# Residual half added on VectorE, plain first gathers, and inverse deviations placed between the second gathers

## What is computed

```python
x = layernorm(x + attention(x))             # causal, ALiBi bias, RMSNorm on q, k and y, then Wproj
logits = x @ w_router                       # 2048 x 8
top_vals, top_idx = top_k(logits, 2)
probs = softmax(top_vals)
for every token and each of its two experts e, with its weight p:
    out += p * (square(relu(x @ w_fc[e])) @ w_proj[e])
x = layernorm(x + out)                      # (v - mean) / sqrt(var + 1e-5)
```

## Time and profile before

| | us |
|---|---|
| median of 3 timed runs | 1530.89 (1529.89 to 1531.99) |
| the profiled execution, its own time | 1529.72 |
| its span in the trace | 1528.0 |
| PE busy in the span | 1430.8 (94%) |
| DVE busy | 770.4 (50%) |
| ACT busy | 728.5 (48%) |
| POOL busy | 421.3 (28%) |
| mean granted TensorE clock | 0.974 of full speed |

### The profile page before, as it was taken

The page is one execution under the profiler, slowest core; times in us unless marked ns, Lnnn a source line. Parts: engine busy times, 40 slices in busy tenths (PEclk is TensorE's granted clock), DMA queues, the critical chain, the costliest instruction groups (busy, mean ns, idle before and its releaser), DMA issues. The chain is left out here.

```text
span 1528.0 us, 26403 instructions
## 1 busy us (share of the span) xinstructions
PE 1430.8 (94%) x8000; PEld 1216.7 (80%) x8001; DVE 770.4 (50%) x1784; ACT 728.5 (48%) x1633; POOL 421.3 (28%) x417
## 2 busy tenths in 40 slices
PE   7999999999999999999999999699999579999980
PEld 5888888888888888888888887588888468888870
DVE  6555555655555655655555555345545433333323
ACT  5655565655655655656555655222222123333333
POOL 1221212212221221221212211143233333443376
PEclk9999999999999999999999999899999789999995
DMA  4112111021111121111111120735455266556499
GB/s 154 51 39 62 35 54 62 28 62 48 41 62 48 41 62 48 41 48 62 41 48 62 37 74 21 271 146 206 160 183 181 102 214 237 202 193 246 138 180 206
DMA packets 71979, 160.24 MB, mean 105 GB/s; under 512 B 14096, under 2 KB 14736, under 8 KB 69520
## 3 DMA queue, kind: packets, MB, share of 16 engines
q1 hardware_dynamic: 61168, 109.56, 21.7%
q0 software_dynamic: 10784, 50.36, 10.9%
HBM read 107.37 MB, written 52.52 MB: 105 GB/s over the span
## 5 line engine op out<-in xcount | busy, mean ns | idle before, releaser
L312 POOL TENSOR_TENSOR small<-small,half 128x4 f32<-128x4 f32 x193 | 194.6, 1008 | 764.5 <-DVE small L341 764.5
L264 ACT ACTIVATE prob<-logit,small 128x128 f32<-128x128 f32 (+3 forms) x256 | 144.2, 563 | 119.7 <-DVE small L413 117.0
L413 DVE CUSTOM_DVE_ANT_0 logit<-score_ps,bias 128x128 f32<-128x128 f32 (+3 forms) x256 | 124.8, 488 | 142.9 <-PE score_ps L506 142.5
L520 PEld LDWEIGHTS y_ps<-vs,prob_t 128*128 128x128 f32 x1280 | 174.8, 191 | 22.4 <-ACT prob_t L271 4.6
L520 PE MATMUL y_ps<-vs,prob_t 128*128 (+1 forms) x1280 | 185.2, 275 | 1.0 <-ACT prob_t L271 0.7
L271 ACT ACTIVATE prob_t<-prob_ps 128x128 f32<-128x128 f32 (+3 forms) x256 | 111.5, 436 | 53.4 <-PE prob_ps L513 52.3
L740 ACT ACTIVATE yt_hi<-turn_ps,subln 128x512 fp32r<-128x512 f32 x64 | 44.0, 688 | 170.4 <-PE turn_ps L1005 166.3
L513 PE MATMUL prob_ps<-ident,prob 128*128 128x128 f32 x640 | 112.7, 274 | 3.2 <-ACT prob L264 3.2
L1014 PE MATMUL out_ps<-w_hi,yt_hi 128*128 128x512 f32 x256 | 107.7, 421 | 6.4 <-DVE yt_lo L846 6.4
L465 PE MATMUL k_ps<-w_hi,x_hi 128*128 (+1 forms) x256 | 103.5, 404 | 6.2 <-DVE w_lo L373 6.2
L465 PE MATMUL v_ps<-w_hi,x_hi 128*128 (+1 forms) x256 | 106.7, 417 | 0.0
(11 more groups left out here) (169 smaller groups left out, 3284.7 us busy)
## 6 DMA issues: line engine op xcount, KB each, us to landing
y_scratch<-x_now SPq DMA_DIRECT2D x65, 256.0 KB, 2.9
x_raw<-in_x_t SPq DMA_DIRECT2D x64, 256.0 KB, 2.8
y_raw<-y_scratch SPq DMA_DIRECT2D x15, 1024.0 KB
w_raw<-in_w_experts POOLq DMA_DIRECT2D x7, 2048.0 KB, 8.3
w_hi<-in_w_experts POOLq DMA_DIRECT2D x7, 2048.0 KB, 8.4
w_raw<-in_w_all SPq DMA_DIRECT2D x16, 768.0 KB, 5.7
slots_y<-zeros SPq DMA_DIRECT2D x13, 768.0 KB
xs<-slots_x SPq DMA_DIRECT2D x39, 256.0 KB
```

Source lines behind the costliest of these rows:

```text
L264: nc.scalar.activation(prob[:, 0:width], logit[:, 0:width], ACT.Exp, scale=-1.0, bias=least[:, h:h + 1], accum_out=row_sum[:, (i % 2) * HG ...
L312: nc.gpsimd.tensor_tensor(r, ms, half[:, :], ALU.pow).then_inc(ready, 1)
L413: nc.vector.tensor_tensor_reduce(out=logit[:, 0:width], in0=score_ps[:, 0:width], in1=bias[:, h, T - width:T], scale=1.0, scalar=3e38, op0 ...
L520: mm = nc.tensor.matmul(y_ps[:, h * D:(h + 1) * D], prob_t[:, j * P:(j + 1) * P], one(vs[:, bass.ds(now, 1), j, h * D:(h + 1) * D]), start ...
```

## The change

Everything is computed at half scale in the resident path, so that the two halves add up in the slot outputs.

- Residual block: POOL's L801 becomes one instruction `(var + eps) * 4`, with a nop before it, so the normalised tile is halved. The `eps` tile and its memset go. The exponential of the second weight takes scale 2, and the gates are multiplied by 4 (through 0.25 in `either`), since the halved input gives a quarter after the square. ACT's copy into `x1` (L747) goes; DVE's `layernorm` waits for `x1_turned` in place of `x1_kept`.
- End of the residual block: dispatch(15) stands before send_gates(14) in POOL's program.
- Expert block: `xs` has four buffers with a semaphore each. The first four row loads wait no more for PE. Later loads are issued after the store of `yo(k)`, where they stood ahead of the wait for it. POOL waits for all four first loads before it goes on to expert 1's `w_hi`.
- ACT's scaled copy into `yo` goes; DVE computes `yo = ye * gate + xs`, last in its step.
- The first gathers have no `compute_op`. The second gathers add as before.
- The inverse deviations are made four tiles at a time after the issue of second gathers 6, 10 and 14, for the tiles 0 to 3, 4 to 7 and 8 to 11, and at the end for 12 and 13, and for 14 and 15. DVE's L1361 follows the same grouping.

```diff
-                out = x1[:, t, :] if isinstance(t, int) else one(x1[:, bass.ds(t, 1), :])
-                nc.scalar.activation(out, x1_now[:, b, :], ACT.Copy).then_inc(x1_kept, 1)
...
-                nc.gpsimd.tensor_tensor(var_eps[:, :], mean_var[:, 1:2], eps[:, :], ALU.add).then_inc(var_biased, 1)
+                pool.nop(nofuse=True)
+                nc.gpsimd.tensor_scalar(var_eps[:, :], mean_var[:, 1:2], EPS, 4.0, ALU.add, ALU.mult).then_inc(var_biased, 1)
...
             dispatch(NT - 2, 0)
+            dispatch(NT - 1, 1)
             send_gates(NT - 2, 0)
-            dispatch(NT - 1, 1)
             send_gates(NT - 1, 1)
...
-        xs = sb("xs", [P, 2, C])
+        xs = sb("xs", [P, YB, C])
...
-                at = tile_at(k)
-                if k >= 2:
-                    sp.wait_ge(xs_turned, k - 1)
-                load_rows(at, k % 2)
+                load_rows(tile_at(k), k)
...
-                if more(k, 4):
-                    sp.wait_ge(xs_turned, k + 3)
-                    sp.nop(nofuse=True)
-                    load_rows(at, b)
                 sp.wait_ge(yo_ready, k + 1)
                 sp.nop(nofuse=True)
                 out = y_slots[k] if isinstance(k, int) else rows_of(y_slots[bass.ds(k, 1), :, :])
                 sp.dma_start(out, yo[:, y, :]).then_inc(yo_stored[y], 16)
                 if more(k, 4):
+                    load_rows(at, y)
                     load_gates(at, y)
...
-            for b in range(2):
-                pool.wait_ge(xs_loaded[b], 16)
+            for y in range(YB):
+                pool.wait_ge(xs_loaded[y], 16)
...
-                                        bass.IndirectOffsetOnAxis(ap=slot_y[:, 0, t:t + 1], axis=0),
-                                        compute_op=ALU.add).then_inc(first_gathered, 16)
+                                        bass.IndirectOffsetOnAxis(ap=slot_y[:, 0, t:t + 1], axis=0))\
+                    .then_inc(first_gathered, 16)
...
+                if t in AFTER:
+                    inverse_std(t - RB - 2, t - 2)
+            for t in (NT - 4, NT - 2):
+                inverse_std(t, t + 2)
...
-                act.wait_ge(down_done, k + 1)
-                act.wait_ge(yo_stored[y], q * 16 + 16)
-                act.wait_ge(g_loaded[y], q * 16 + 16)
-                nc.scalar.activation(yo[:, y, :], ye_ps[b][:, :], ACT.Copy, scale=gs[:, y:y + 1]).then_inc(yo_ready, 1)
...
+                dve.wait_ge(down_done, k + 1)
+                dve.wait_ge(yo_stored[y], q * 16 + 16)
+                dve.wait_ge(g_loaded[y], q * 16 + 16)
+                nc.vector.scalar_tensor_tensor(yo[:, y, :], ye_ps[b][:, :], gs[:, y:y + 1], xs[:, y, :],
+                                               ALU.mult, ALU.add).then_inc(yo_ready, 1)
```

More of the change, by code:

```diff
@@ L752, in second_weight @@
                 src = gap[:, t:t + 1] if isinstance(t, int) else gap[:, bass.ds(t, 1)]
-                nc.scalar.activation(second[:, b:b + 1], src, ACT.Exp).then_inc(second_ready, 1)
+                nc.scalar.activation(second[:, b:b + 1], src, ACT.Exp, scale=2.0).then_inc(second_ready, 1)
             act.wait_ge(early_loaded, 32)
@@ L1118, in expert_phase @@
         we_loaded = sem("we_loaded")
-        xs_loaded = [sem("xs_loaded0"), sem("xs_loaded1")]
+        xs_loaded = [sem(f"xs_loaded{y}") for y in range(YB)]
         xs_turned, xt_rounded, xt_ready = sem("xs_turned"), sem("xt_rounded"), sem("xt_ready")
@@ L1247, in _, with inverse_std @@
                 pool.indirect_dma_start(x1[:, t, :], None, slots_y,
[L1248 to L1249 removed]
+                                        bass.IndirectOffsetOnAxis(ap=slot_y[:, 0, t:t + 1], axis=0))\
+                    .then_inc(first_gathered, 16)
             stored_up_to(E - 1)
             pool.wait_ge(first_gathered, 16 * NT)
+            def inverse_std(first, last):
+                pool.wait_ge(var_biased, last)
+                nc.gpsimd.tensor_tensor(rstd[:, first:last], var_eps[:, first:last], half[:, 0:last - first], ALU.pow)\
+                    .then_inc(rstd_ready, last - first)
+            pool.wait_ge(set_up, 1)
             for t in range(NT):
@@ L1255, in _ @@
                                         compute_op=ALU.add).then_inc(second_gathered[t], 16)
-            pool.wait_ge(set_up, 1)
-            for t in range(NT):
-                if t % 2 == 1 and t < NT - 2 or t >= NT - 2:
-                    n = 2 if t < NT - 2 else 1
-                    part = slice(t + 1 - n, t + 1)
-                    pool.wait_ge(var_biased, t + 1)
-                    nc.gpsimd.tensor_tensor(rstd[:, part], var_eps[:, part], half[:, 0:n], ALU.pow)\
-                        .then_inc(rstd_ready, n)
+                if t in AFTER:
+                    inverse_std(t - RB - 2, t - 2)
+            for t in (NT - 4, NT - 2):
+                inverse_std(t, t + 2)
         @block.scalar
@@ L1357, in bias_variance, with scale_mean @@
                     .then_inc(var_biased, 1)
-            def scale_mean(t):
-                dve.wait_ge(rstd_ready, t + 1)
-                nc.vector.scalar_tensor_tensor(minus_mean[:, t:t + 1], mean_var[:, t, 0:1], -1.0, rstd[:, t:t + 1],
-                                               ALU.mult, ALU.mult).then_inc(mean_ready, 1)
+            def scale_mean(first, last):
+                dve.wait_ge(rstd_ready, last)
+                nc.vector.scalar_tensor_tensor(minus_mean[:, first:last], mean_var[:, first:last, 0], -1.0,
+                                               rstd[:, first:last], ALU.mult, ALU.mult).then_inc(mean_ready, last - first)
             for t in range(NT):
@@ L1373, in _, with turn_x @@
             bias_variance(NT - 1)
-            for t in range(NT - 3, NT):
-                scale_mean(t)
+            for t in (NT - 4, NT - 2):
+                scale_mean(t, t + 2)
         @block.tensor
         def _(pe):
-            def turn_x(b, loaded):
-                pe.wait_ge(xs_loaded[b], loaded)
+            def turn_x(b, y, loaded):
+                pe.wait_ge(xs_loaded[y], loaded)
                 for c in range(CT):
-                    mm = nc.tensor.transpose(xt_ps[b][:, c * P:(c + 1) * P], xs[:, b, c * P:(c + 1) * P], ident[:, :])
+                    mm = nc.tensor.transpose(xt_ps[b][:, c * P:(c + 1) * P], xs[:, y, c * P:(c + 1) * P], ident[:, :])
                 mm.then_inc(xs_turned, 1)
```

37 lines of the change are left out of this document (18 added, 19 removed).

## The result

The changed kernel takes 1550.61 us (median of four runs, 1549.22 to 1554.26), the kernel before 1531.44 beside it: a ratio of 1.0136 with an interval of 1.0123 to 1.0149. It is 1.3% slower where 0.2% faster was forecast, and outside the range. The profiled execution has a span of 1547.6 against 1528.0, 19.6 more.

What follows compares the result with a forecast made beforehand. PE was taken to bound nearly everything, gathers and statistics the last 46 us. Slots 5.2 us later (2.5 + 2.7), yet second gathers 3.9 earlier; with 0.4 more tail, -3.5 us in sum: 1527.4 us, range 1523.5 to 1533.

Steps and rivals of the forecast that it cites:

- meeting point: End of the residual block: two POOL DMAs moved behind dispatch(15) make POOL's wait there end 2.5 us later.
- `w_hi`(1) late, with the boundary: Start of the expert block: POOL's wait for four row loads issues expert 1's `w_hi` 7.6 us late, plus the boundary's 2.5.
- chain late at expert 5, with the boundary: POOL's weight chain recovers 2.4 us and is 5.2 us late at expert 5, plus the boundary's 2.5.
- PE's stall for `w_lo` at tile 22: Expert 5's first tile: PE has 2.2 us of slack and stands 2.7 us for the late low parts.
- waits for rows: SP's later row loads in the slot steps: cost taken as 0, bound 1.5 us.
- tile 31 stored late: Slot tiles at the end of the expert block: 5.2 us late, from 2.5 at the boundary and 2.7 of PE's stall.
- plain gather, step: First gathers on POOL: 1.3 us a step without the addition, bounds 1.3 and 1.85.
- slot steps beside the gathers: Last slot tiles while POOL issues first gathers: no added time was counted.
- store of tile 35 to second gathers: The store of tile 35 ends last ahead of the second gathers, which start 2.89 us after it.
- tail: Start of the second gathers to the end: 46.6 us against 46.2, three POOL pauses included; bounds 45.5 and 49.
- dear plain gathers: Rival: POOL's plain first gathers cost as much as adding ones, 1.85 us each; say 1535.1 us, chance 0.13.
- DVE's addition: DVE's three-operand operation in each slot step: 0.75 us, hidden; without cover 0.75 on each of 39 tiles.

Runs made afterwards that it cites:

- a_freewait: The changed kernel with a wait that is always met ahead of every first gather; 1539.54 us in one run.
- b_plain: The kernel before with one edit, first gathers without the addition (residual missing from the result); 1537.35 us, ratio 1.0051.
- a_win8_alone: The changed kernel with one edit: first gather t waits until gather t-8 has landed; 1540.08 us in one run.
- a_onewait: The changed kernel with a single wait, ahead of first gather 8, for the landing of gather 0; 1537.78 us in one run.
- b_half: The kernel before with plain first gathers that bring rows of half the width; span 1520.2 us in one run.
- b_tail: The kernel before with inverse deviations for six, four and three tiles behind second gathers 10, 13 and 15, then one and two; 1528.64 us, ratio 0.9987.
- a_win4: The changed kernel with first gather t waiting for gather t-4's landing, gates of tile 14 before dispatch(15), a wait for two row loads and b_tail's grouping; 1525.02 us, ratio 0.9955.
- a_paced: The changed kernel with a one-column power on POOL behind each plain first gather, 1.86 us a step; 1538.65 us, ratio 1.0051.
- a_pace_short: The changed kernel with a 0.2 us sum on POOL behind each plain first gather, 1.37 us a step; 1550.84 us, ratio 1.0129.
- a_burst4: The changed kernel, but after every fourth first gather POOL waits until all issued ones have landed; 1547.27 us in one run.
- a_order: The changed kernel with send_gates(14) ahead of dispatch(15) again, as before the change; 1548.36 us, ratio 1.0112.
- a_win6: As a_win4, but first gather t waits until gather t-6 has landed; 1525.37 us in one run.
- a_win8: As a_win4, but first gather t waits until gather t-8 has landed; 1524.49 us in one run.
- a_nowin: a_win8 without its waits between the first gathers, its other edits kept; 1529.39 us in one run.
- a_add: The changed kernel with adding first gathers again, onto zeros that ACT writes; 1541.9 us, ratio 1.0070.

## Why the prediction was wrong

| step | forecast | measured |
|---|---|---|
| meeting point | +2.5 | +3.1 |
| `w_hi`(1) late, with the boundary | 10.1 | 10.9 |
| chain late at expert 5, with the boundary | 7.7 | 9.6 |
| PE's stall for `w_lo` at tile 22 | 2.7 | 1.8 (PE's bracket: 1.57) |
| waits for rows | 0 | 2.1 and 0.6 |
| tile 31 stored late | 5.2 | 8.0 (11.2 to 13.9 in six others) |
| plain gather, step | 1.3 | 1.26 |
| slot steps beside the gathers | unchanged | +14.4 |
| store of tile 35 to second gathers | 2.9 | 2.9 |
| tail | 46.6 | 52.5 |

Added up against the forecast's span (1528.0 - 3.5 = 1524.5): 2.8 for the slots ahead of the gathers, 14.4 for the standstill and 5.9 for the tail are 23.1, and 1524.5 + 23.1 = 1547.6. In a_freewait, without the standstill, the excess over the forecast is 13.3 us: 6.9 for the slots, 0.9 between the store of tile 35 and the second gathers, 5.5 for the tail (52.1). So the forecast fails with and without the standstill.

- *What held.* The rival "dear plain gathers" was wrong: they take 0.95 us, and b_plain shows the same. The end of the wait at the meeting point does follow the last issue: 7.1 us, where I took 6.1. What ends last ahead of the second gathers is the store of tile 35, as I said. DVE's addition takes 0.75 and is hidden in the slot steps (not at their end, see the tail). The Trainium skill's rule (page "SBUF — State Buffer", "Who interferes with whom"), by which a VectorE instruction with at most one SBUF input, outside the two-port modes, does not contend with GpSimd, agrees with the traces: POOL's eight subtractions take 10.5 to 10.9 us in the changed kernel and took 10.5 to 11.0 in the kernel before (10.49 is that of the earlier trace rows).
- *The step that failed first.* "Slots are 5.2 late at the end" took it that plain gathers do nothing to PE. I priced only what they cost POOL, and no bound was set for what they do to others. The trace of before could not have shown it: its adding gathers go beside slot tiles too, at a higher DMA share, with PE busy throughout:
```profile
1447.00:1478.00 31.00, 31.00 (x156) 25.64 (x155) 9.92 (x15) 10.98 (x20) 25.14 (x16) 1.00 0.98 186
```
This window of before leaves no sign that a gather could hold PE. The standstill is 14.4 of the 23.1 us, and why it comes is open. a_win8_alone, a_onewait and a_freewait, in which it is missing, still take 1537.8 to 1540.1, some 7 to 9 us over before. By them the sign of my forecast would have been wrong too.
- *The tail, a term mis-sized by 5.9* (46.6 forecast, 52.5 measured, outside its bounds of 45.5 and 49). I let tile 4's statistics start when its second gather lands. But DVE runs in program order, and in the changed kernel its scaling of tiles 36 to 38 stands ahead of all statistics. PE makes tile 38 ready 16.6 us after tile 35 is stored, and the second gathers start 2.9 after that store: the statistics can't start before about 13.7 us into the tail. The first power began 18.5 us into it and not 13.6 as forecast. The three pauses cost 6.7, 3.3 and 2.4 us where 2.5, 2.4 and 2.3 were forecast, so the first alone is 4.2 of the 5.9. The rows for it were there (tiles 35 to 38 are stored over 17.9 us). While the pace of the gathers held the second ones back in the kernel before, this didn't show; the change moves them up to the slot tiles, and by its own addition makes DVE wait for the last down-projection. (In b_half, where ACT still scales, DVE's statistics start 10.6 us into the tail; in a_freewait and the changed kernel 13.5 and 14.4.) b_tail and a_win4, which ask for the first power only behind gather 10, show 44.1 and 44.2.
- *Rows, a term mis-sized.* I gave SP's later loads 0 with a bound of 1.5. They cost 2.7, 2.1 in the step of tile 4 (of which 1.23 stand in PE's bracket) and 0.6 in that of tile 10. I had 8.1 us of room and 8.6 for the worst load, and called the difference a few tenths. The load behind the 2.1 is that of tile 6's rows: issued at 1262.50, just behind a 2 MB weight load of 1261.85, it landed at 1271.73, after 9.2 us. SP now issues it only behind the store of tile 2.
- *The spread that I didn't see.* The 8.0 us at tile 31 are those of one execution, the fastest of the changed kernel's four. In a_paced, a_pace_short, a_burst4, a_win8_alone, a_onewait and a_freewait, whose programs are the same up to the gathers, tile 31 is stored 11.2 to 13.9 us late, by waits for rows at changing tiles and mostly longer losses at tile 21. So the term "5.2 late" was too small by 2.8 to 8.7.
- *Weight chain.* The direction and place were right. It recovered 1.3 us by expert 5 where I counted 2.4, but PE had lost 2.7 to rows by then, and so waited less.

## What to carry to other kernels

When an edit frees a resource that held others back, write down for each engine what stands ahead, in its program, of the first thing that the earlier start now asks of it: here DVE's last slot tiles made the first pause of the tail 4.2 us longer than forecast. Losses that are caught by the same later wait (late weights, late rows, a late start) need not add, and need not come back one by one: of the 3 us that a_order gave back at its place 0.5 were left one wait later, part of it lost to the clock behind that wait. Don't judge such a change from one pair of traces when kernels with the same program differ by more than its worth. A limit on how many gathers may be outstanding costs nothing where they land in time (a_win6, a_win8); that it prevents a standstill is not shown, since a_nowin without it did not stand still either.

## What the runs showed that I had not expected

- PE's signals of finished matmuls came 10.5 to 13.9 us late, all at once, beside plain indirect gathers of 256 KB every 1.26 us, in the changed kernel and in much the same way in four others; at 1.37 us a step they came late in several bouts. At 1.86 us a step, or with adding gathers, beside them on the same chip never. All six traces also lack most of the landing signals of these gathers. The cause is open.
- A plain gather of 128 rows takes POOL 0.95 us, an adding one 1.54; the DMA engines bring plain ones every 1.26 us beside the slot tiles at a share of 0.77 and 250 GB/s. Adding ones every 1.88 fill the share to 0.98 at 186 GB/s.
- POOL's wait at the end of the block grows by more than the issues moved behind the last dispatch: 9.4 to 10.2 us with the old order (b_plain 9.5, a_nowin 10.2), 12.3 to 13.7 with four gate scatters in a row.
- POOL's sequencer runs ahead of its gathers: in a_win8 it was at the wait ahead of gather 8 while gather 2 was being issued.
- PE's waits of 1.84 us (a_paced) and 2.49 us (a_order) ahead of tile 22 were followed by 3.4 us at the lower granted clock; those of 1.57 (the changed kernel), 2.13 (a_onewait) and 3.19 us (a_add) at the same place were not.
